# An octonion feed-forward kernel: the product h is written in f32 straight to SBUF, and its high and low halves are taken from there

## The reference

```
y    = einsum('bct,bcd->bdt', x, W_cond[itok])            # 32 x 64 rows of 1024
gate = oct_ternary_linear(y, w_gate)                       # 8 x 341 hidden
up   = oct_ternary_linear(y, w_up)
h    = silu(gate) * up
out  = x + oct_ternary_linear(h, w_down)

def oct_ternary_linear(xp, W):       # W is (8, out/8, in/8)
    scale = mean(|W|); Wq = scale * clip(round(W / scale), -1, 1)
    M = einsum('jik,jod->koid', S_OCT, Wq)                 # octonion signs
    return einsum('...id,koid->...ko', xp, M)
```

## Time and profile before

| | us |
|---|---|
| median of 3 executions | 768.2 (767.93 to 768.47) |
| the profiled execution, its own time | 768.18 |
| its span in the trace | 766.4 |
| PE busy | 692.2 (90%) |
| VectorE busy | 519.6 (68%) |
| GpSimd busy | 422.2 (55%) |
| ScalarE busy | 336.3 (44%) |
| DMA, mean over the span | 41 GB/s |

### The profile page before, as it was taken

How to read it: one execution, slowest core, us unless ns; L and a number is a source line. 1 busy time by engine, 2 the same in 40 slices (tenths; PEclk the granted TensorE clock), 3 DMA queues, 4 the chain that set the end, 5 groups by cost and what they waited for, 6 DMA issues and landing times.

```text
span 766.4 us, 16879 instructions
## 1 busy us (share of the span) xinstructions
PE 692.2 (90%) x6934; PEld 624.8 (82%) x6934; DVE 519.6 (68%) x830; ACT 336.3 (44%) x529; POOL 422.2 (55%) x448
## 2 busy tenths in 40 slices
PE   4259959899998999899998999899998999989994
PEld 3248948799897999789897999789897998988893
DVE  2859648566875678566875678566884668567846
ACT  4434746144452555245452554335451545334531
POOL 0200996664766356664766456764666347864560
PEclk9569989999999999999999999999999999999998
DMA  8200010031000210021000310021100300011001
GB/s 247 107 1 20 38 59 3 2 110 58 3 2 28 84 59 1 2 91 62 19 2 2 111 59 2 1 85 32 56 1 2 110 2 1 2 59 53 1 2 56
DMA packets 16703, 31.32 MB, mean 41 GB/s; under 512 B 3314, under 2 KB 10482, under 8 KB 16626
## 3 DMA queue, kind: packets, MB, share of 16 engines
q1 hardware_dynamic: 16626, 30.24, 11.9%
HBM read 21.84 MB, written 8.39 MB: 39 GB/s over the span
## 4 chain that ended last, share of the span: by engine, by line
PE 60%; POOL 19%; issue 9%; DVE 5%; ACT 5%; SPq 1%; DMA 0%; DVEq 0%; POOLq 0%
PE ps L918 49%; POOL z_f L505 8%; POOL h_pairs L505 8%; PE ps L995 7%; PE ps L905 3%; DVE z_op L780 2%; ACT z_op L606 2%; POOL down_u L505 2%; POOL z_op L505 1%; ACT h_op L591 1%; PE ps L912 1%; DVE o_sb L421 1%; POOL y_f L505 1%; ACT h_f L594 1%; DVE u_sb L785 1%
## 5 line engine op out<-in xcount | busy, mean ns | idle before, releaser
L918 PE MATMUL ps<-y_op,gate_table 128*128 128x256 f16 x2112 | 273.5, 275 | 13.7 <-DVE h_op L775 8.7
L918 PE MATMUL ps<-y_op,up_table 128*128 128x256 f16 x2112 | 271.9, 274 | 2.7 <-DVE up_table L718 2.7
L918 PEld LDWEIGHTS ps<-y_op,gate_table 128*128 128x128 f16 x2112 | 208.1, 99 | 39.8 <-DVE h_op L775 9.2
L918 PEld LDWEIGHTS ps<-y_op,up_table 128*128 128x128 f16 x2112 | 207.5, 98 | 28.1 <-DVE up_table L718 3.2
L505 POOL TENSOR_TENSOR h_pairs<-h_f 128x256 f32<-128x256 f32 x144 | 149.9, 1069 | 104.1 <-ACT h_f L594 100.3
L505 POOL TENSOR_TENSOR z_f<-h_pairs 128x512 f32<-128x512 f32 x96 | 129.7, 1372 | 99.2 <-DVE z_op L780 96.6
L618 ACT ACTIVATE ps<-ps,small 128x512 f32<-128x512 f32 x96 | 63.6, 662 | 164.3 <-DVE ps L785 122.8
L780 DVE TENSOR_TENSOR z_op<-z_f,z_op 128x1024 f16<-128x1024 f32 x48 | 61.8, 1288 | 86.9 <-ACT z_op L606 86.9
L995 PE MATMUL ps<-down_u,z_op 128*128 128x256 f16 x768 | 97.1, 285 | 19.6 <-DVE z_op L780 19.6
L421 POOL TENSOR_TENSOR o_sb<-o_sb,wd_sb 128x256 f32<-128x256 f32 (+1 forms) x140 | 81.6, 620 | 51.8 <-DVE wd_sb L830 50.7
L995 PEld LDWEIGHTS ps<-down_u,z_op 128*128 128x128 f16 x768 | 76.6, 102 | 31.9 <-DVE z_op L780 20.8
(11 more groups left out here) (72 smaller groups left out, 438.9 us busy)
## 6 DMA issues: line engine op xcount, KB each, us to landing
x_in<-in_x_dram SPq DMA_DIRECT2D x8, 1024.0 KB, 5.1
o_sb<-in_x_dram SPq DMA_DIRECT2D x16, 512.0 KB, 3.7
out_dram<-o_sb SPq DMA_DIRECT2D x16, 512.0 KB, 2.7
h_op<-in_L_ffn_w_gate_dram SPq DMA_DIRECT2D x3, 512.0 KB, 5.5
h_op<-in_L_ffn_w_up_dram SPq DMA_DIRECT2D x3, 512.0 KB, 5.5
z_op<-in_L_ffn_w_down_dram SPq DMA_DIRECT2D x1, 1364.0 KB, 9.2
cond_bd<-in_L_cond_weights_dram SPq DMA_DIRECT2D x32, 16.0 KB, 2.9
idx_sb<-in_itok_B_dram SPq DMA_DIRECT2D x1, 0.1 KB
```

The source lines that it names most:

```text
L918: mm = pe.matmul(dst, table[m][:, slot, q, :], y_op[:, op, e, :], start=(i == 0 and e == 0), stop=(i == len(terms) - 1 and e == 1))
```

## The change

The product on VectorE writes h_f in SBUF instead of the bank. ScalarE's second reading of the bank falls away with its semaphore h_copied. ScalarE's high half and VectorE's low half read h_f. The wait that keeps h_f from being overwritten while GpSimd still needs it, and the wait for the transposition in tile 0, move from ScalarE to VectorE. The banks are now free when the product has been made, so TensorE's waits go by h_ready.

```diff
             def round_of_z(T, k):
                 n = NR * T + k
-                pool.wait_ge(h_copied, NC * T + 4 * (k // 2) + 4)
+                pool.wait_ge(h_ready, NC * T + 4 * (k // 2) + 4)
...
             def split_h(T, c):
-                n, s = NC * T + c, c % 2
+                n = NC * T + c
                 act.wait_ge(h_ready, n + 1)
                 if T > 0 and c == 0:
                     act.wait_ge(down_u_done, SUB * T)
                 if T == 0 and c == 0:
                     act.wait_ge(tern_ready, 2)
-                    act.wait_ge(transposed, 2 * NQ)
-                act.activation(h_op[:, c, :, 0, :], bank_r(s, 0), ACT.Copy).then_inc(h_hi_ready, 1)
-                if T > 0 and c % 4 == 0:
-                    act.wait_ge(pairs_ready, NR * (T - 1) + 2 * (c // 4) + 2)
-                act.activation(h_f[:, c], bank_r(s, 0), ACT.Copy).then_inc(h_copied, 1)
+                act.activation(h_op[:, c, :, 0, :], h_f[:, c], ACT.Copy).then_inc(h_hi_ready, 1)
...
             def h_lo(T, c):
                 dve.wait_ge(h_hi_ready, n + 1)
-                dve.wait_ge(h_copied, n + 1)
-                dve.tensor_tensor(h_op[:, c, :, 1, :], bank_r(s, 0), h_op[:, c, :, 0, :], ALU.subtract
+                dve.tensor_tensor(h_op[:, c, :, 1, :], h_f[:, c], h_op[:, c, :, 0, :], ALU.subtract
                                   ).then_inc(h_lo_ready, 1)
...
                 dve.wait_ge(silu_ready, n + 1)
                 dve.wait_ge(u_ready, n + 1)
-                dve.scalar_tensor_tensor(out=bank_r(s, 0), in0=u_sb[:], scalar=up_scale(T), in1=bank_r(s, 0),
+                if T > 0 and c % 4 == 0:
+                    dve.wait_ge(pairs_ready, NR * (T - 1) + 2 * (c // 4) + 2)
+                if T == 0 and c == 0:
+                    dve.wait_ge(transposed, 2 * NQ)
+                dve.scalar_tensor_tensor(out=h_f[:, c], in0=u_sb[:], scalar=up_scale(T), in1=bank_r(s, 0),
                                          op0=ALU.mult, op1=ALU.mult).then_inc(h_ready, 1)
...
         own(T, c), m == 0:
-                            pe.wait_ge(h_lo_ready, n - 1)
-                            pe.wait_ge(h_copied, n - 1)
+                            pe.wait_ge(h_ready, n - 1)
...
         down(T):
-                    pe.wait_ge(h_lo_ready, done - 1 + s)
-                    pe.wait_ge(h_copied, done - 1 + s)
+                    pe.wait_ge(h_ready, done - 1 + s)
+                    pe.wait_ge(h_lo_ready, done - 4)
```

More of the change, by code:

```diff
@@ L372, in build @@
         h_hi_ready = sem("h_hi_ready")
-        h_copied = sem("h_copied")
         h_lo_ready = sem("h_lo_ready")
```

## The result

The changed kernel takes 780.5 us (779.57 to 780.97, 4 runs) against 768.34 us: the ratio is 1.0157 with a 95% interval of 1.014 to 1.0175, so it is slower by 12.2 us. The forecast was 774.8 us, the range ended at 780.0. The direction was right, the size was half of what came, and the range was missed by 0.5 us.

A forecast was written before the change was run, and what follows sets the result against it. TensorE, busy 90%, was the bound, idling chiefly in seven tile-end waits set by GpSimd's chain. The 768.2 us before plus 4.6 for these waits and 2.0 for tile 0 gave 774.8 us, range 764 to 780.

The forecast's parts named there:

- Step 1: Tile's end: chunk 10's low half on VectorE is blocked by GpSimd's z_f(3), making chunk 11's product 0.8 us late.
- Step 2: Tile's end: GpSimd starts round 4 of z once the product is there, 0.6 us earlier than before.
- Step 3: GpSimd's round 4: 5.42 us alone, plus clashes with z_lo(3) 0.95, chunk 11's low half 0.4, split of y 3.37.
- Sum per tile +0.65: TensorE's wait at a tile's end grows by about 0.65 us, seven times: +4.6 us.
- Tile 0, +2.0: First tile: low halves beside busy GpSimd cost +2.0 us, between -2 and +4.
- The +1.4 from GpSimd's weights: Tile 0: low halves of chunks 3, 4 and 5 hold up GpSimd's down weights, 3 x 0.45 = +1.4 us on z_hi(0).
- The 0.6 for the low halves after them: Tile 0, VectorE's chunks 7 to 11: further low halves beside busy GpSimd cost 0.6 us for the lot.
- z_hi(0) after 103: Sign that the forecast is right: in tile 0, ScalarE's z_hi(0) comes after 103 us.
- The row norms' wait: Tile 0: TensorE's wait for the low half goes; one for the row norms' squares from ScalarE takes its place.
- The last tile gives and takes nothing: The last tile has no such gap at its end (7 waits for 8 tiles), so about nothing changes.
- I leave it at 4: Slow-clock last down products stay at 4 of 7, 1.66 us each; a count of 0 to 7 would give -6.6 to +5.0.
- More dips: Part of the forecast's 0.64 chance: some 0.15 for more slow-clock last down products, to 780 us.

The follow-up runs named there:

- run 5: Changed kernel, but chunk 10's low half alone in each tile takes its first input from the PSUM bank (wrong values there): 769.8 us.
- run 10: Changed kernel with VectorE's split of the next tile's y moved from ahead of z_lo(4) to behind z_lo(5): 750.17 us.
- run 3: Kernel before, with six small one-column VectorE instructions ahead of the last z_lo of tiles 0 to 6: 773.65 us.
- run 4: Kernel before, with twelve small one-column VectorE instructions ahead of the last z_lo of tiles 0 to 6: 777.62 us.
- run 6: Changed kernel with 28 TensorE products with zeros in the wait at the end of tiles 0 to 6: 768.74 us.
- run 7: Kernel before with 23 TensorE products with zeros in each of the seven waits at a tile's end: 760.97 us.
- run 9: Kernel before with VectorE's split of the next tile's y moved from ahead of z_lo(4) to behind z_lo(5): 742.64 us.
- run 1: Changed kernel, but every low half reads the PSUM bank (wrong values) and TensorE again waits for the low half before reusing a bank: 760.67 us.
- run 2: Kernel before with one line of the change: the low half reads h_f in SBUF instead of the bank: 781.93 us.
- run 8: Changed kernel, but in tile 0 alone the low halves read the bank (wrong values) and TensorE waits for them there: 775.48 us.

## Why the prediction came out as it did

*The bound, the chain, the rows to look at*: right. The changed kernel's loss sits in the seven waits and in tile 0.

*The low half alone takes as long from SBUF as from PSUM, the product and the high half cost nothing*: right; where no GpSimd instruction is beside it, a low half takes 0.68 to 0.69, the high half +0.03 us (632 against 599).

*Step 1, the low half of chunk 10 blocked, product 0.8 us late*: right. From the start of chunk 10's u sum to the end of chunk 11's product it is 6.73 us (302.08 to 308.81) where the earlier trace rows and the same span of before give 5.97: +0.76. Run 5 takes that one clash away and 0.76 us of wait with it.

*Step 2, GpSimd 0.6 us early*: right (0.66 by the same measure). *Step 3, round 4 at 5.42 + 0.95 + 0.4 + 3.37 = 10.14*: measured 10.15. *Sum per tile +0.65*: measured +0.70 in six tiles; the steps as written add up to +0.75 (314.7 against 313.99), so the 0.65 was a slip, of 0.7 us over seven tiles. The Trainium skill's rule (SBUF — State Buffer, Who interferes with whom), cited there for the sign, also holds in its detail, see below.

*Tile 0, +2.0 and its +0.65*: 2.40 measured. The +1.4 from GpSimd's weights was 1.34. The 0.6 for the low halves after them was 0.4 by run 10's rows; in the profiled execution it was 1.4, with 1.05 given back by an early start that has nothing to do with the change. So the sign "z_hi(0) after 103" failed (102.04) though the term held; run 10 has it at 103.21. The row norms' wait came as forecast.

*The last tile gives and takes nothing*: +0.3.

**The step that failed is the clock, "I leave it at 4".** The prediction had read that four of seven tiles dip behind waits of 2.8 us. It let the count go from 0 to 7 "when gaps and periods shift", had each gap grow in its own sum, and still put this term at nothing, without a reason. Runs 3 and 4 lengthen this wait alone, and the count grows; runs 6 and 7 fill it, and the count falls to none. The profiled executions, one for each kernel, by length of the wait and number of slow last products of seven:

```
kernel                         wait us      slow of 7
no wait (runs 9, 10), 0.3 (7), 0.45 (6)         0
run 1                          2.3              2
run 5                          2.75             3
before                         2.8              4
run 3                          3.17             6
run 2                          3.2              7
after                          3.5              6
run 8, tiles 1 to 6            3.5              5 of 6
run 4                          3.5              7
```

With this the term was 2 or 3 dips, 3.3 to 5 us, not 0; profiled, 4.45, of the 4.8 us by which this execution (779.57) lies over the forecast. More dips had been given 0.15 of the forecast's 0.64 (to 780), where they were the likeliest case. The median of the changed kernel is another 0.9 us over the profiled execution. A seventh dip for some executions would do that, and so might another meeting in tile 0 (chunk 9's low half took 1.76 us here, 1.41 in run 6, 0.68 in run 10); no trace of those executions is kept.

## What to carry to other kernels

Before a VectorE operand moves from PSUM to SBUF, look at what GpSimd does in that stretch: an instruction with two SBUF inputs cost GpSimd 0.94 to 0.97 ns per element here and may itself wait for a whole GpSimd instruction, and one such meeting on the critical chain outweighs a removed copy on an idle engine. A wait of TensorE is worth more than its length: price it with the slow products behind it, or fill it with harmless products. And where two engines clash on the chain, first look for work there that could be done later: moving the split of y was worth 25.7 us, the planned saving at best 7.7.

## What the hardware showed beyond that

VectorE is blocked for the whole of GpSimd's instruction, not slowed; the 0 to 1.1 us that the prediction allowed for it was too short. In tile 0 of the changed kernel a low half starts 0.05 us behind a long one of GpSimd:

```profile
76.29 3.09 POOL L504 TENSOR_TENSOR z_op<-z_op 128x1536 f16<-128x1536 f16 x1
76.34 3.59 DVE L769 TENSOR_TENSOR h_op<-h_f,h_op 128x512 f16<-128x512 f32 x1
```

It ends at 79.93, 0.55 us after GpSimd's end at 79.38, which is its own data time (512 elements at 1.04 ns), so it had waited for nearly all of the 3.09 us. By the Trainium skill's rule (SBUF — State Buffer, Who interferes with whom) that the earlier one holds the interface for its whole instruction, the trace agrees.

The length of TensorE's idling does not decide a dip alone: in tile 0 of run 1 a wait of 2.12 us was followed by products at full clock, in tile 0 of run 8 one of 2.13 us by slow ones, and the kernel before dips behind four of seven waits of the same 2.8 us. Ahead of the last products no wait of 0.46 us or less was followed by a dip, nor were the two longer ones, 0.95 (tile 0 of run 10) and 1.26 (tile 0 of run 6); between that and 2.12 us there was none.
